# The small job of each attention unit moved behind its value products

## What is computed

```
out = x + attention(xn) + experts(xn)

attention: 8 heads of width 8 for queries, keys and values
  qk = xn @ Wqk.T + bqk         (queries and keys interleaved, 64 + 64 columns)
  v  = xn @ Wv.T + bv
  a  = softmax(q @ k.T) / 8     (per batch and head, 512 x 512)
  attention = (a @ v) @ Wo.T + bo

experts: 8 experts, the 2 with the largest logits of xn @ W_gate + b_gate
  y  = relu(xn @ W_e + b_e), mean over the token's two experts
```

## Time and profile before

| | us |
|---|---|
| median of 3 runs | 321.46 (320.15 to 325.24) |
| the profiled execution | 321.12 |
| its span | 319.4 |
| TensorE busy (share of the span) | 298.2 (93%) |
| VectorE | 218.1 (68%) |
| ScalarE | 167.3 (52%) |
| GpSimd | 193.8 (61%) |

### The profile page before, as it was taken

The page is one execution under the profiler, slowest core; times in us unless marked ns, Lnnn a source line. Parts: engine busy times, 40 slices in busy tenths (PEclk is TensorE's granted clock), DMA queues, the critical chain, the costliest instruction groups (busy, mean ns, idle before and its releaser), DMA issues.

```text
span 319.4 us, 5521 instructions
## 1 busy us (share of the span) xinstructions
PE 298.2 (93%) x1711; PEld 195.0 (61%) x1711; DVE 218.1 (68%) x465; ACT 167.3 (52%) x250; POOL 193.8 (61%) x212
## 2 busy tenths in 40 slices
PE   7777999998999999999999999999899999999983
PEld 2466887976877777777777777777333333333332
DVE  3888877865866667766766686666468898884144
ACT  0677975802443222324432223342998978878950
POOL 4278790069996666698557765435547888886000
PEclk9999999869999999999999999999999999999999
DMA  7799999533446444443443444411699999999323
GB/s 221 259 399 336 358 292 411 228 88 110 133 132 196 134 132 132 134 132 134 132 131 131 134 160 140 131 59 47 192 314 263 145 197 203 152 210 197 71 98 133
DMA packets 29404, 57.51 MB, mean 180 GB/s; under 512 B 4928, under 2 KB 5056, under 8 KB 29248
## 3 DMA queue, kind: packets, MB, share of 16 engines
q1 hardware_dynamic: 19264, 37.49, 32.8%
q0 software_dynamic: 7728, 18.62, 27.7%
q10 hardware_dynamic: 2384, 1.04, 1.2%
HBM read 38.52 MB, written 18.61 MB: 179 GB/s over the span
## 4 chain that ended last, share of the span: by engine, by line
PE 70%; DVE 10%; POOL 8%; issue 4%; ACT 3%; ACTq 2%; DVEq 0%; POOLq 0%
PE ps_l L1200 28%; PE ps_o L1140 7%; PE ps_l L1057 7%; PE ps_l L1129 6%; PE ps_r L1111 5%; PE ps_l L1178 5%; DVE row_max L913 4%; POOL row_in L515 4%; PE ps_r L1087 3%; PE ps_r L1148 2%; PE ps_l L1042 2%; POOL row_mid L531 2%; ACT probs L704 2%; PE ps_r L1099 2%; POOL lay L349 1%
## 5 line engine op out<-in xcount | busy, mean ns | idle before, releaser
L1200 PE MATMUL ps_l<-w_split,t_hi 128*128 x312 | 100.1, 402 | 1.1 <-ACT t_hi L656 1.1
L913 DVE TENSOR_REDUCE row_max<-ps_r 128x1 f32<-128x512 f32 x128 | 82.3, 683 | 10.7 <-PE ps_r L1111 10.6
L661 ACT ACTIVATE row_mid<-row_mid 128x512 f32<-128x512 f32 x39 | 24.6, 632 | 102.1 <-DVE row_mid L934 102.1
L531 POOL TENSOR_TENSOR row_mid<-row_mid,bias_o 128x512 f32<-128x512 f32 x39 | 50.9, 1304 | 44.0 <-ACT row_mid L661 43.8
L704 ACT ACTIVATE probs<-ps_l 128x1024 f32<-128x1024 f32 x64 | 64.2, 1031 | 11.2 <-PE ps_l L1129 10.9
L1200 PEld LDWEIGHTS ps_l<-w_split,t_hi 128*128 128x128 f32 x312 | 55.7, 188 | 11.5 <-issue 1.6
L1200 PE MATMUL ps_l<-w_split,t_lo 128*128 x156 | 61.1, 392 | 0.0
L564 POOL DMA_INDIRECT acc<-expert_rows,slots_i x32 | 49.8, 1556 | 17.3 <-issue 8.8
L934 DVE TENSOR_TENSOR row_mid<-ps_l,bias_e 128x512 f32<-128x512 f32 x39 | 27.0, 692 | 41.5 <-PE ps_l L1200 41.5
L515 POOL DMA_INDIRECT row_in<-xn_rows,gather_i x39 | 40.7, 1044 | 23.8 <-DVE gather_i L878 17.5
L1111 PE MATMUL ps_r<-k_t,q_t 32*128 32x512 f32 x128 | 41.0, 491 | 0.6 <-DVE row_max L913 0.5
(11 more groups left out here) (169 smaller groups left out, 407.1 us busy)
## 6 DMA issues: line engine op xcount, KB each, us to landing
expert_rows<-row_mid SPq DMA_DIRECT2D x39, 256.0 KB, 2.0
w_split<-in_L_ffn_W_e_dram SPq DMA_DIRECT2D x8, 512.0 KB, 6.4
xn_rows<-row_mid SPq DMA_DIRECT2D x16, 256.0 KB, 6.6
w_split<-in_L_ffn_W_e_dram SPq DMA_DIRECT2D x4, 1024.0 KB, 9.5
acc<-in_L_attn_x_dram SPq DMA_DIRECT2D x16, 256.0 KB, 5.4
out_dram<-res SPq DMA_DIRECT2D x16, 256.0 KB, 3.0
row_in<-in_L_attn_x_dram SPq DMA_DIRECT2D x8, 256.0 KB, 5.5
w_split<-in_L_attn_x_dram SPq DMA_DIRECT2D x8, 256.0 KB, 9.5
```

The source lines that it names most:

```text
L531: pool.tensor_tensor(row_mid[:, n % 4, :], row_mid[:, n % 4, :], bias_o[:], ALU.add).then_inc(y_done, 1)
L913: dve.tensor_reduce(row_max[:, b % 2, h, i:i + 1], ring_bank(item), AX.X, ALU.max).then_inc(freed_by_dve, 1)
L1200: mm = pe.matmul(ps_y[:, n % 2, :], a[:, n % 2, ks], rhs, start=(k == 0), stop=(k == 3 * KC - 1))
```

## The change

Each unit's job moves behind the value products. TensorE had: first pair, its scores, job, second pair, its scores, value products. It now has: first pair, its scores, second pair, its scores, value products, job. The ring's list has the job behind both halves' scores. ScalarE copies a kept job after both exponentials in place of after the first; VectorE serves its jobs after the maxima of both halves in place of after those of the first. `keep_o` still follows all of these. No instruction is added or taken away, and the tail isn't touched.

```diff
--- before.py
+++ after.py
@@ -277,7 +277,7 @@
         for b in range(B):
             for u in range(2 * HG):
                 t = 2 * (2 * HG * b + u)
-                ring += half_scores[t] + unit_jobs(b, u) + half_scores[t + 1]
+                ring += half_scores[t] + half_scores[t + 1] + unit_jobs(b, u)
         ring_no = {item: n for n, item in enumerate(ring)}
         KEPT = ("k", "q", "max", "turn")
         score_no = {item: n for n, item in enumerate(item for item in ring if item[0] == "score")}
@@ -702,10 +702,9 @@
 
                             act.wait_ge(pv_done, n - 1)
                         act.activation(probs[:, n % 2, 2 * half:2 * half + 2, :], logit_pair(half), ACT.Exp).then_inc(exp_done, 1)
-                        if half == 0:
-                            for job in unit_jobs(b, u):
-                                if job[0] in KEPT:
-                                    keep(*job)
+                    for job in unit_jobs(b, u):
+                        if job[0] in KEPT:
+                            keep(*job)
                     if u == 0 and b >= 1:
                         keep_o(b - 1, 1)
                     if u == HG:
@@ -987,8 +986,7 @@
                             maximum(item)
                             if item == group_scores[item[1], item[2] // HG][-1]:
                                 lay_max(item[1], item[2] // HG)
-                        if half == 0:
-                            serve(unit_jobs(b, u))
+                    serve(unit_jobs(b, u))
 
             def lay_half(piece):
 
@@ -1213,13 +1211,13 @@
                     logits(b, u, 0)
                     for item in half_scores[2 * n]:
                         scores(item)
-                    for job in unit_jobs(b, u):
-                        fill(*job)
                     logits(b, u, 1)
                     for item in half_scores[2 * n + 1]:
                         scores(item)
                     if n >= 1:
                         values(*divmod(n - 1, 2 * HG))
+                    for job in unit_jobs(b, u):
+                        fill(*job)
             values(B - 1, 2 * HG - 1)
             for kind, part in TAIL:
                 if kind == "o":
```

## The result

The changed kernel takes 324.42 us (median of 20 runs, 321.61 to 327.53) against 321.54 (320.02 to 325.24, 20 runs). The ratio is 1.0063, with a 95% interval of 1.0039 to 1.0087: 2.0 us slower, within 2%. The forecast was 1.4 us slower, 322.8, with 318.3 to 327.5 as its range.

The account below looks back on a forecast made before the run. TensorE's own order was taken to set a unit, with nothing having much slack. The terms, +1.6 - 0.9 + 1.1 + 1.3 - 1.7 + 0.5 - 0.5 = +1.4 us, gave 322.8 us, range 318.3 to 327.5.

Parts of the forecast that it names:

- Third score behind product, sums or both: Next unit's third score waits for the job's bank: +0.2 behind products or sums, +0.3 behind both; +1.6 together.
- Behind kept jobs: Units 2, 3, 4, 12 and 20: third score stalls 0.3 for the bank of a job ScalarE copies, net 0.
- ScalarE's queue: Value products of units 5, 9, 17 wait for sums copied behind a kept job, +1.1; second pairs of 6, 10, 18, +1.3.
- Units 6, 8 and 18: They follow a unit without a job and gain 0.29 each, -0.9; second pairs of 6 and 18 wait 0.43 for exponentials.
- Waits on maxima that go: Jobs at the unit's end no longer wait on VectorE's maxima for their bank: -1.7 us.
- VectorE's lag: VectorE, working in order, lags where laying out maxima falls beside two jobs: nothing to 1.0, taken as +0.5 us.
- Units 24 to 30: In units 24 to 31, without scores, three intervals of product units at the end gain 0.18 each: -0.5 us.
- a unit with two scores: With two scores each pair takes 0.43 in either order, so putting the pairs side by side gains nothing.
- The step that was missing is the clock: The granted clock was read as 1.00, the 2.4 GHz level, throughout and given no part in the forecast.
- the wait lies open in full: Rival, chance 0.20: the late third score undoes the packing, so stalls count whole, +5.4, or 326.9 us.
- the packing wins: Rival, chance 0.15: third scores don't wait, 15 job units with three scores gain 0.29 each; -6.6, or 314.9 us.
- everything shifts alike: Rival, chance 0.10: producer and consumers move together, VectorE sets the unit in both orders; 321.5 us, within 1 either way.

Follow-up runs that it names:

- experiment 4: The changed kernel with five matmuls in unit 0 whose result nobody reads, three ahead of the second pair, two behind the job: 322.30 us, ratio 1.0004.
- experiment 5: The kernel before with three unread matmuls behind the second pair of unit 0: 319.96 us, ratio 0.9941; second run 320.16 us, ratio 0.9987.
- experiment 9: The kernel before with three unread matmuls in unit 0 and only sums, turns and products moved behind the value products: 321.26 us, ratio 0.9978.
- 10: The changed kernel with the job ahead of the value products, same ring order, and five unread matmuls in unit 0: 323.1 us, ratio 1.0069.
- experiment 1: The changed kernel with unit 0's job back between its two pairs: 326.57 us, ratio 1.0127.
- experiment 2: The kernel before with only unit 0's job moved behind the second pair: 321.27 us, ratio 0.9983.

## Why the prediction was right

Its direction and size held, and most of its steps did, though several terms were off in both directions and cancelled. The sizes below are the distances between unit starts in experiment 4 against those in the second run of experiment 5, both with the clock at 1.00 throughout, so that the clock takes no part.

- **Third score behind product, sums or both.** In units 13, 16, 22 and 23 the distances rose by 0.21, 0.31, 0.00 and 0.23. In 21, 11 and 15 they rose by 0.03, 0.09 and 0.13, but there a job's wait on a maximum went as well (0.23, 0.37 and 0.51 us in the profile before), so the third scores cost some 0.26, 0.46 and 0.64. That is 2.1 in all for a forecast of 1.6. Units 11 and 15 were dearer than worked out; unit 22 came out at nothing because its third score waited for a result already in the kernel before, which the working didn't take off.
- **Behind kept jobs** (2, 3, 4, 12, 20), forecast 0: +0.36.
- **ScalarE's queue**, units 5, 9 and 17, forecast +1.1: 0.45 + 0.45 + 0.46 = +1.36. Unit 10, forecast +0.4: +0.34; it takes as much in experiment 9, where no job stands ahead of a copy, so that part isn't the queue's alone. Units 6, 8 and 18, forecast 0 on balance (packing against exponentials): +0.32.
- **Waits on maxima that go**, forecast -1.7: the four of the profile before, in units 11, 15, 19 and 21, came to 0.37 + 0.51 + 0.62 + 0.23 = 1.73, and in the rows by line above the jobs have 0.0 of idle time left. Three units got shorter: 19 by 0.86 (0.62 of it this wait), 14 by 0.21 and 7 by 0.25 (there the idle time ahead of its third score fell from 0.46 to 0.21). VectorE's lag, forecast +0.5, shows nowhere by itself.
- Units 2 to 23 in all: forecast +1.9, measured 62.30 - 60.24 = **+2.06**. Units 24 to 30, forecast -0.5: 16.68 - 17.08 = -0.40.

So the mechanism was right, and that the sum came out within 0.2 is partly luck: the third scores (+0.5), the kept jobs (+0.4) and ScalarE (+0.5) cost more, and the lag (-0.5), the units of two scores (-0.45) and unit 7 (-0.25) less. Counted from unit 3 to the start of unit 31, experiment 4 is 1.6 and the profile after 1.2 over the old order.

One step was wrong, and its harm was hidden by the others: a unit with two scores was said to gain nothing from pairs side by side. It gains 0.2, which is all that unit 14 gained and the rest of what unit 19 did. The profile after, unit 14, has 0.66 from the first pair to the value products against the 0.86 of two slots:

```profile
263.62 0.50 PE L1127 MATMUL ps_l<-q_t,k_t 32*128 32x512 f32 x2
264.28 1.04 PE L1138 MATMUL ps_o<-probs,proj 128*9 128x512 f32 x8
```

This is the direction in which the rule of the Trainium skill points that the prediction cites (TensorEngine Tiling (Array Packing), section Key Properties: a change of tiling mode drains TensorE). The trace agrees in the direction, by this 0.2; that a drain is the cause, no run here shows. It was right of the matmuls and still no guide to the time.

**The step that was missing is the clock.** "The granted clock is 1.00 (the 2.4 GHz level) throughout, so it has no part here" held for the profile before and not for the changed kernel. Over the 20 listed runs of the changed kernel time and clock go together: 321.61, 321.82 and 322.12 us at a mean clock of 0.988, 0.989 and 0.986, and 324.4 to 324.7 mostly at 0.976 or 0.977. Time lost to the clock, span times (1 - clock), is on average 7.0 us in the changed kernel and 6.5, 6.2 and 6.1 in the kernel before in the three series; a line through the 29 runs of the first of these gives 0.60 us of time for each us so lost. By that, which is an estimate across series, 0.4 of the 2.0 us are the clock's and 1.6 the order's, which fits the traces. The forecast's 1.4 was for the order alone.

The rivals: that the wait lies open in full (326.9) was too dear: the twelve units that it counted cost 2.5 (the 2.1 and 0.36 above) and not 5.1, and unit 13 came out at 2.98 from fill to fill. That the packing wins was refuted by experiments 4 and 10. That everything shifts alike (321.5) falls with the traces, where the changed order is slower by more than executions of one order differ. Why the copies cost 0.3 more than worked out, and the third scores of units 11 and 15 together 0.6 more, was not tried.

## What to carry to other kernels

Moving a job on one engine moves it in every ring and every queue in which it stands. Ask what the third item behind it is in a ring of three banks, and what stands behind its copy on the emptying engine; here these two took back more than the 0.3 us a unit that the matmuls gained. And a job that looks like a mere interruption may be what keeps TensorE busy at a change of stage: look at the clock there in several executions, since one profile can miss its fall.

## What the runs showed of the hardware

TensorE's granted clock halved at 226.15 in the changed kernel, behind idle stretches of 0.68 and 0.49 us, and at 225.44 in experiment 1, behind one of 1.07. It did not fall behind 0.67 and 0.49 us in experiment 2, nor behind the 1.07 us of the profile before, although in both TensorE's work was the same as in the execution that fell until less than 0.1 us before the fall. It stayed at half for 6.8 us in the first and 13.7 us in the second, although TensorE was busy all the time from 227 and 228 on.

Five unread matmuls in that place, about 1.7 us of work in idle time, raised the mean clock of the changed kernel from 0.978 to 0.988; its mean time is 322.2 after 324.0, in different series.
